# Masked MLP: weight loads into the ring issued by ScalarE, and a threshold search paced to end four slots ahead of the down stage

## The reference, cut to what matters

```python
s = silu(x @ w_gate.T)                       # 2048 x 1376
_, idx = top_k(-abs(s), 688)                 # the 688 smallest magnitudes of each row
s[rows, idx] = 0
out = (s * (x @ w_up.T)) @ w_down.T
```

## Time and profile before

| what | us |
|---|---|
| median of 3 runs | 1975.94 |
| the runs | 1975.94, 1987.93, 1972.41 |
| the profiled execution, device time | 1980.81 |
| its span, first to last instruction | 1979.0 |
| attention and projection, up to the first statistics of the MLP phase | about 676 |
| one FFN stage / one gate stage, undisturbed | 52.22 / 30.59 |

### The profile page before, as it was taken

How to read it: one execution, slowest core, us unless ns; L and a number is a source line. 1 busy time by engine, 2 the same in 40 slices (tenths; PEclk the granted TensorE clock), 3 DMA queues, 4 the chain that set the end, 5 groups by cost and what they waited for, 6 DMA issues and landing times.

```text
span 1979.0 us, 39339 instructions
## 1 busy us (share of the span) xinstructions
PE 1836.3 (93%) x14968; PEld 1122.2 (57%) x14968; DVE 1462.5 (74%) x2302; ACT 1031.1 (52%) x1888; POOL 760.7 (38%) x922
## 2 busy tenths in 40 slices
PE   7998888888889798999999998999999999989979
PEld 3443333333333476775775766666676766747746
DVE  6567688888873313997988988887889889969821
ACT  4234677777774123654654645636646546536411
POOL 4685656566772111223215224142151151322331
PEclk9998899999999898999999999999999999999989
DMA  7864544556434604006132331234232142071010
GB/s 237 233 198 139 153 120 126 141 140 182 142 110 118 207 1 126 12 12 188 36 125 50 81 125 41 90 81 143 68 105 73 40 133 73 12 201 33 12 40 12
DMA packets 217131, 205.68 MB, mean 104 GB/s; under 512 B 136400, under 2 KB 173264, under 8 KB 216992
## 3 DMA queue, kind: packets, MB, share of 16 engines
q1 hardware_dynamic: 210992, 187.77, 33.3%
q0 software_dynamic: 4272, 12.91, 2.0%
q10 hardware_dynamic: 1728, 3.15, 0.4%
HBM read 147.39 MB, written 33.62 MB: 91 GB/s over the span
## 4 chain that ended last, share of the span: by engine, by line
PE 51%; DVE 6%; issue 3%; POOL 3%; DMA 2%; ACT 1%; SPq 0%; DVEq 0%; ACTq 0%
PE ga L1507 12%; PE ub L1507 12%; PE acc L1517 12%; PE ga L1535 5%; PE ub L1535 5%; PE acc L1550 4%; DVE junk L1651 1%; DMA pp<-ax 1%; POOL ax L1469 1%; POOL pp L1463 1%; DVE kept L1701 1%; DVE h L1708 1%; POOL lohi L1453 1%; DMA ring<-wgu_scr 0%; DVE pat L1655 0%
## 5 line engine op out<-in xcount | busy, mean ns | idle before, releaser
L1453 POOL TENSOR_TENSOR lohi<-h,lohi 128x256 f16<-128x256 f32 x224 | 176.4, 788 | 737.8 <-ACT lohi L1598 737.6
L1587 ACT ACTIVATE kept<-ax,T 128x1376 f16<-128x1376 f32 x248 | 357.0, 1439 | 170.5 <-DVE T L1657 166.7
L1651 DVE TENSOR_SCALAR_CACHE_REDUCE junk<-ax,T 128x1376 f16<-128x1376 f32 x248 | 406.4, 1639 | 3.3
L1067 ACT ACTIVATE pr<-s 128x512 f32<-128x512 f32 (+2 forms) x640 | 320.2, 553 | 96.1 <-PE s L956 75.5
L649 DVE TENSOR_REDUCE mx<-s 128x2 f32<-128x1024 f32 (+2 forms) x300 | 319.9, 1113 | 65.3 <-PE s L628 34.7
L1507 PE MATMUL ga<-xT_f,w_gate 128*128 128x256 f16 x2688 | 332.8, 274 | 17.8 <-DVE h L1708 13.6
L1507 PE MATMUL ub<-xT_f,w_up 128*128 128x256 f16 x2688 | 332.6, 274 | 0.0
L1517 PE MATMUL acc<-w_down,lohi 128*128 128x512 f16 x1344 | 326.4, 379 | 3.9 <-POOL lohi L1453 3.9
L1507 PEld LDWEIGHTS ga<-xT_f,w_gate 128*128 128x128 f16 x2688 | 262.7, 98 | 95.0 <-DVE h L1708 21.3
L1507 PEld LDWEIGHTS ub<-xT_f,w_up 128*128 128x128 f16 x2688 | 264.3, 98 | 31.6
L1708 DVE SCALAR_TENSOR_TENSOR h<-ub,g 128x256 f32<-128x256 f32 x224 | 93.8, 419 | 155.0 <-ACT g L1593 154.0
(11 more groups left out here) (179 smaller groups left out, 2670.5 us busy)
## 6 DMA issues: line engine op xcount, KB each, us to landing
ring<-wgu_scr SPq DMA_DIRECT2D x64, 688.0 KB, 5.3
ring<-wd_scr SPq DMA_DIRECT2D x24, 768.0 KB, 6.1
wgu_scr<-tk_h POOLq DMA_DIRECT2D x32, 172.0 KB, 2.7
q_scr<-qk_h SPq DMA_DIRECT2D x16, 256.0 KB, 2.5
k_scr<-qk_h SPq DMA_DIRECT2D x16, 256.0 KB, 4.0
v_scr<-v_f SPq DMA_DIRECT2D x16, 256.0 KB, 5.1
Q<-q_scr SPq DMA_DIRECT2D x64, 64.0 KB, 2.1
K<-k_scr SPq DMA_DIRECT2D x64, 64.0 KB, 2.0
```

The source lines that it names most:

```text
L1067: nc.scalar.activation(pr[:, g % NPR, NP * t + p0:NP * t + p1, 0:w], scores, ACT.Exp, scale=SCALE).then_inc(e2_ok, 1)
L1453: nc.gpsimd.tensor_tensor(hT[j % 2][:, 1, :], h[j % 2][:, :], hT[j % 2][:, 0, :], ALU.subtract).then_inc(hl_ok, 1)
L1587: nc.scalar.activation(kept[0][:, :], ax[k % 2][:, 1, 0:I_TK], ACT.Sign, scale=-1.0, bias=TF[:, 1:2], accum_out=cnt[:, 1:2]).then_inc(c1_o ...
L1651: nc.vector.tensor_scalar(junk[:, :], ax[k % 2][:, 0, 0:I_TK], TF[:, 0:1], -float(KZERO), ALU.is_lt, ALU.add, accum_out=cnt[:, 0:1]).then_ ...
```

## The change

The functions `load_g` and `load_d` move, unchanged but for the engine, from SyncE's program to ScalarE's. ScalarE issues the first four loads at the start of the phase, and afterwards the loads of a slot behind that slot's unit, Signs and norm halves and ahead of its `masked_highs`. SyncE keeps transpositions, stores and loads of X. In the planner, the last four slots ahead of a down stage are not counted instead of the last two, so that a higher rate is asked for; and three of the small items are priced anew: 31 at 150 instead of 80, 38 and 39 at 150 instead of 250. Worked through with these numbers, item 37 and item 48 (the ends of the two masks) fall into these slots:

| chunk | before: 37, 48 | after: 37, 48 |
|---|---|---|
| 0 | f1 of chunk 2, slot 13; gates 1, slot 5 | slot 12; slot 3 |
| 1 | f2 of chunk 0, slots 3 and 7 | slots 3 and 7 |
| 2 | gates 3, slot 6; f2 of chunk 1, slot 3 | slot 5; slot 1 |
| 3 | f1 of chunk 5, slot 13; gates 4, slot 5 | slot 12; slot 3 |
| 4 | f1 of chunk 6, slots 3 and 7 | slots 3 and 6 |
| 5 | gates 6, slot 5; f1 of chunk 7, slot 3 | slot 4; slot 1 |
| 6 | f2 of chunk 4, slot 13; gates 7, slot 5 | slot 11; slot 3 |
| 7 | f2 of chunk 6, slots 8 and 11 | slots 6 and 9 |

```diff
--- before.py
+++ after.py
@@ -1387,29 +1387,6 @@
                 sp.dma_start(X[:, c % XR, :, :], x1_scr[c * CW:(c + 1) * CW, :].rearrange("(t p) d -> p t d", p=P)
                              ).then_inc(x_in[c % XR], 16)
 
-            def load_g(k, f):
-                c, m, r = f // 2, f % 2, f % RING
-                if f >= RING:
-                    wait(sp, gm_ok, GU * k + TPC * (c - 1))
-                elif k == 1:
-                    wait(sp, gm_ok, TPC * ((f + RING) // 2 + 1))
-                elif k > 1:
-                    wait(sp, dm_ok, DU * (k - 2) + DG + f + 1)
-                sp.dma_start(ring[r][:, 0:2 * KB * TKW], wgu_scr[m, c].rearrange("p a k w -> p (a k w)")
-                             ).then_inc(ring_in[r], 16)
-
-            def load_d(k, d):
-                if k + 1 < NC:
-                    wait(sp, gm_ok, GU * (k + 1) + TPC * (3 + d // 2))
-                else:
-                    wait(sp, dm_ok, DU * (k - 1) + DG + d + 1)
-                full = min(DB, TKB - 1 - DB * d)
-                sp.dma_start(ring[d][:, 0:full * 2 * D].rearrange("p (j w) -> p j w", j=full),
-                             wd_scr[DB * d:DB * d + full].rearrange("j p a d -> p j (a d)")).then_inc(ring_in[d], 16)
-                if full < DB:
-                    sp.dma_start(ring[d][0:ROWS_LAST, full * 2 * D:(full + 1) * 2 * D],
-                                 wd_scr[TKB - 1, 0:ROWS_LAST].rearrange("p a d -> p (a d)")).then_inc(ring_in[d], 16)
-
             def turn_masked(k, t):
                 sp.wait_ge(pad_ok, 4 + TPC * k + t + 1)
                 sp.wait_ge(ml_ok, 2 * (TPC * k + t + 1))
@@ -1424,18 +1401,12 @@
 
             for c in range(XR):
                 load_x(c)
-            for f in range(RING):
-                load_g(0, f)
             for s in stages:
                 for slot in s.slots:
                     for u, t in slot.shifts:
                         norms[u.name].shift(sp, u, t)
                     for k, t in slot.masked_turns:
                         turn_masked(k, t)
-                    for k, f in slot.gate_loads:
-                        load_g(k, f)
-                    for k, d in slot.down_loads:
-                        load_d(k, d)
                     for done in slot.stores:
                         store(done)
                     for c in slot.refills:
@@ -1577,6 +1548,29 @@
         def _(act):
             nc.scalar.preload_act_table(ACT.Silu)
 
+            def load_g(k, f):
+                c, m, r = f // 2, f % 2, f % RING
+                if f >= RING:
+                    wait(act, gm_ok, GU * k + TPC * (c - 1))
+                elif k == 1:
+                    wait(act, gm_ok, TPC * ((f + RING) // 2 + 1))
+                elif k > 1:
+                    wait(act, dm_ok, DU * (k - 2) + DG + f + 1)
+                act.dma_start(ring[r][:, 0:2 * KB * TKW], wgu_scr[m, c].rearrange("p a k w -> p (a k w)")
+                             ).then_inc(ring_in[r], 16)
+
+            def load_d(k, d):
+                if k + 1 < NC:
+                    wait(act, gm_ok, GU * (k + 1) + TPC * (3 + d // 2))
+                else:
+                    wait(act, dm_ok, DU * (k - 1) + DG + d + 1)
+                full = min(DB, TKB - 1 - DB * d)
+                act.dma_start(ring[d][:, 0:full * 2 * D].rearrange("p (j w) -> p j w", j=full),
+                             wd_scr[DB * d:DB * d + full].rearrange("j p a d -> p j (a d)")).then_inc(ring_in[d], 16)
+                if full < DB:
+                    act.dma_start(ring[d][0:ROWS_LAST, full * 2 * D:(full + 1) * 2 * D],
+                                 wd_scr[TKB - 1, 0:ROWS_LAST].rearrange("p a d -> p (a d)")).then_inc(ring_in[d], 16)
+
             def signs(k, i):
                 if i:
                     act.wait_ge(u_ok, NBITS * k + i)
@@ -1614,6 +1608,8 @@
                 act.wait_ge(hm_ok, 2 * (TPC * k + t + 1))
                 nc.scalar.activation(halves[k % 2][:, t, 0, 0:I_TK], pp[k % 2][:, t, 0:I_TK], ACT.Copy).then_inc(mh_ok, 1)
 
+            for f in range(RING):
+                load_g(0, f)
             norms["f1"].on_scalar(act, first)
             for s in stages:
                 for n, slot in enumerate(s.slots):
@@ -1629,6 +1625,10 @@
                         signs(k, i)
                     for u in slot.highs:
                         norms[u.name].high_half(act, u)
+                    for k, f in slot.gate_loads:
+                        load_g(k, f)
+                    for k, d in slot.down_loads:
+                        load_d(k, d)
                     for k, t in slot.masked_highs:
                         masked_high(k, t)
                 if s.kind == "gates":
@@ -1897,7 +1897,7 @@
 
     spans = {"f1": 3860, "f2": 3860, "gates": 3460, "down": 1950}
     evictions = {"f1": 430, "f2": 430, "gates": 530, "down": 0}
-    costs = [2450] * N_BITS + [80, 1740, 150, 950, 3180, 1650, 1900, 250, 250, 1740, 150, 150, 1740, 150, 950, 3180,
+    costs = [2450] * N_BITS + [150, 1740, 150, 950, 3180, 1650, 1900, 150, 150, 1740, 150, 150, 1740, 150, 950, 3180,
                                1650, 1900]
     first, last = at["gates", 0] + 1, at["down", NC - 1]
     own = [(p, slot, spans[s.kind], evictions[s.kind] + 700 * len(slot.taken) + 1800 * len(slot.stats)
@@ -1908,7 +1908,7 @@
     for n, (p, slot, span, duty) in enumerate(own):
         rate = 0
         for k in range(NC):
-            ahead = [(l, d) for q, _slot, l, d in own[n:] if q < at["down", k]][:-2]
+            ahead = [(l, d) for q, _slot, l, d in own[n:] if q < at["down", k]][:-4]
             left = sum(costs[item] for c, item in items if c <= k)
             if left and ahead:
                 rate = max(rate, (left + sum(d for _l, d in ahead)) / sum(l for l, _d in ahead))
```

## The result

The changed kernel takes 2007.74 us (median of 4 runs, 2005.83 to 2015.07) against 1974.18 before (4 runs, 1969.32 to 1987.93): a ratio of 1.0166, 95% interval 1.0141 to 1.0191. I had forecast 1959.

What follows compares the result with a forecast made beforehand. TensorE, busy 93% of the span, was taken as the bound, leaving only its waits and slow clock to win. Terms -13.3 + 0.5 - 5.9 + 2 - 1 + 0.7 = -17.0 us gave 1963.8 from 1980.8, or 1959 from the median; range 1945 to 1979.

Steps and rivals of the forecast that it cites:

- signs of being wrong: Gates 2 or 5 above 31 us, masked FFN stages above 60, last overlapped FFN stage over 3 us idle.
- A, the down stages: Gate and down stages of chunks 1, 4, 7: ScalarE's loads gain 13.3 us (7 to 18), 3 lost per pair.
- A, gates 0, 2, 3 and 5: Gate stages 2 and 5: a Sign ahead of ScalarE's load costs 0.5 us for both (0 to 3).
- C: Chunks 1 and 4: items 31 and 32 move to the last gate slot, 2 us of loss (0 to 5).
- E: Start of phase: ring loads share transfers with the first X, 0.5 us lost; 0.2 for fuller FFN ends.
- B: End, chunk 7: earlier masks remove 7.4 us, ScalarE's wait costs 1.5; net gain 5.9 (4.8 to 7.4).
- D: Chunks 2 and 5: tile 1's mask leaves POOL's low-half slots; gain 1 us (gain 4 to loss 5).
- the loads land late all the same: Last four gate units: three transpositions and four loads whoever issues; half of A stays, 1965 us; chance 0.12.
- Only moved: A's idle time returns in FFN stages because VectorE gets the same work into less time; 1970 us; chance 0.20.
- ScalarE late with the ring: Gate stages: ScalarE issues pairs later than 3.0 us after the unit, TensorE idles; +24 us, 2000; chance 0.08.

Runs made afterwards that it cites:

- both mended: Kernel before with new planner; SyncE issues loads first, next unit's transpositions last in gates 1, 4, 7; f2 0 and f1 6 items from 38 in old slots: 1955.75 us.
- pace alone: Kernel before with the new planner (four-slot cut, new prices), ring loads still issued by SyncE: 1987.25 us, ratio 1.0050.
- issuer alone: Changed kernel with the old planner, so ScalarE issues the ring loads but the search is paced as before: 1995.94 us, ratio 1.0102.
- loads first: Kernel before, SyncE issuing ring loads ahead of transpositions in gates 1, 4, 7: 1971.89 us; the same order with the new planner: 1966.33 us.

## Why the prediction was wrong

The sum had -17.0; the profiled MLP phase has +34.8. Two of the signs of being wrong came up: gates 2 and 5 are above 31 us, f2 0 and f1 6 above 60. Of the 51.8 us between:

- **A, the down stages: 25.2.** The gate stages went nearly as I said (30.59 in gates 4 and 7; the load of gates 1 is issued at 904.17, 0.5 us after SiLU began, earlier than my 1.2 us behind the unit). Gates 1 keeps 1.7 us, 1.25 of them a wait for VectorE's product pp that every run with the new pace has and that I had not seen. The step that failed is "1.2 us to the issue and 4.5 to 6.1 to the landing [...] leave 1.8 to 3.4 us idle". I took both ends from loads that stand behind one another on SyncE's queue; on a second queue beside the masked transposition they took 14 to 16 us in down 0. I had seen that item 48 moves to slot 3, and followed its train to ScalarE's copy, but not to the transposition in slot 6. The three pairs of stages gave +11.9 where I had -13.3; with the old pace, and so without that meeting, they give -6.8.
- **A, gates 0, 2, 3 and 5: 13.6.** I looked there for a Sign ahead of a load (0.5 us), and the loads were in time. The transpositions were not. SyncE's order, which I read as the fault in gates 1, 4 and 7, was in gates 2, 3 and 5 what kept the transpositions ahead of the loads.
- **C: 10.4.** "VectorE may be late by hardly one block" took items 31 and 32 for the whole edit. For these two it was right: in *both mended* they stand where the change puts them, and the two stages take 113.1 us against 112.7. Earlier finishing items also pull the next chunk's search forward, into a stage where VectorE is busy 51.16 of 56.88 us; +14.8 in the two stages, -2.4 in the down stages behind them, against my 2. About 4.9 of it (the windows of the pace alone set against the changed kernel's: 60.63 to 61.65, 61.90 to 65.83) goes with the slower clock behind the wait for the transposition: TensorE's busy time in the two stages is 7.6 us longer there, its waits are shorter.
- **E: 3.0.** "A shared transfer can delay it" was right, its size not: 3.0 us against 0.5, beyond the bound of 2. The other 0.5 lies in the stages f1 0 to f1 2 (0.7 against 0.2).
- **B: 1.5.** The wait of 5.90 went, as I said, but in f2 5 and f2 6 TensorE now waits 2.65 us for h and POOL's low halves, where I had 1.5 for ScalarE's wait: -4.4 against -5.9, just outside the bounds of 4.8 to 7.4.
- **D: -1.9.** It held in size, -2.9 against -1, with gates 6 longer by 2.4 us and the FFN stages shorter. The wait in gates 6 (2.21 us) ended with the transposition, as I said, and within 0.1 us of it with VectorE's product pp, which I had not named.

Of the rivals, "the loads land late all the same" was nearest: it named three transpositions and four loads in the last four gate units. But I let it only eat half a gain, as if the load could be no later than before, and let the transposition pay nothing. "Only moved" named VectorE, which, as far as its busy time tells, decided C. "ScalarE late with the ring", the one that I had on the slower side, fell: no gate stage of the changed kernel waits for a gate load (with the issuer alone gates 7 has one wait, of 1.35 us).

## What to carry to other kernels

One queue is also an order of priority: before moving loads to another issuer, list the small urgent transfers that stood ahead of them and ask who waits for those. What a second issuer was to bring in the gate and down stages came from the order on the first, together with the new pace: loads whose place is free first, the next stage's transpositions last (142.7 us for the three pairs, against 156.9). And when a pace is raised to clear one wait, look at what moves up behind the work that you meant to move.

## What the runs showed of the hardware

- Two transpositions alone at the head of a queue land in 2.8 us; beside two loads of 768 KB on another queue in 8.3 (8.0 with the issuer alone); behind two such loads on their own queue in 7.2 and 7.9.
- The masked transposition of tile 1 and the last down loads took, from first issue to last landing, 9.7 us on one queue with the loads first (918.16 to 927.9), 13.3 with the transposition first (916.95 to 930.3), 19.1 on two queues (916.20 to 935.25, the landing of the last load's second piece). The Trainium skill, "DMA: Bandwidth & Descriptors", section "Issuing engines are not separate DMA queues", says that all issuers' transfers share the same engines, so I would expect equal totals; gate stage 2 agrees (9.9 against 9.5), this place does not: with both under way the queues moved 0.73 MB in 6 us. Why stays open.
- A transposition holds its issuing engine. Two of the norm with no load under way held SyncE 2.59 us (gates 2 of the kernel before); behind two loads on SyncE's queue 6.52, and beside two loads on ScalarE's 6.69 (gates 2 of the changed kernel). The larger masked one held it 2.79 us in gates 4 of the kernel before and 8.20 in gates 7 with the loads first.
